# A feature-interaction tower: product arrays halved twice by accumulating DMAs, with gathers, diagonals and adds placed anew

## The chip, the cores and the metric

One core of a Trainium2 chip runs the whole program. The metric is the device time of one launch in microseconds. The kernel before takes 673.68 us, the median of three runs (673.07 to 673.69).

## What is computed

The reference looks up 39 embeddings of 16 numbers for each of 512 samples, runs three compressed-interaction layers over them, and a small network on top:

```
e  = stack(tbl_f[ids[:, f]] for f in 0..38)            # 512 x 39 x 16
X1 = einsum('hjk,bjd,bkd->bhd', W0, e, e)  + b0        # 512 x 128 x 16
X2 = einsum('hjk,bjd,bkd->bhd', W1, e, X1) + b1
X3 = einsum('hjk,bjd,bkd->bhd', W2, e, X2) + b2
z  = concat(X1.sum(2), X2.sum(2), X3.sum(2))           # 512 x 384
h  = relu(concat(z, dense_ctx) @ W_top1 + b_top1)      # 400 -> 512
h  = relu(h @ W_top2 + b_top2)                         # 512 -> 256
y  = h @ W_top3                                        # 512 x 1
```

Only the sum of X3 over d is needed, so the kernel never forms X3: it forms, for each sample, the products of x0 and X2 summed over d (called G, 39 rows and a row of plain sums), and applies W2 to those once at the end.

## The kernel before, in words

The 512 x 16 pairs of sample and d are 8192 columns. They are worked off in 16 **groups** of 512 columns (32 samples), each of four **tiles** of 128 columns (8 samples). The work of a group has two parts, and the engines run them a group apart.

**Getting embeddings and X1, one group ahead.** GpSimd adds table offsets to the ids (`index`, L317) and issues ten indirect DMAs (`gather`, L324) that fetch the rows of a group into one half of `emb`. SP (`x0_of`, L275) waits until all ten have landed, stores the rows to DRAM (L245), reads them back transposed as `rep` (L255), waits for this, and copies `rep` onto further partitions (L259). Then `factors` (L261) loads three copies as the first factor of the pair products (L268) and, one after another as VectorE uses them up, six second factors (L273), all into `shared`. SP does this in one queue in the order factors(g), x0_of(g+1), factors(g+1). While the engines work on group X, VectorE forms the seven pair products of group X+1 (`form_pairs`, L653) after the chunks in `FORM_AT` (the 7th, 11th, ... of the group's 40), TensorE multiplies them with the weights five chunks later (`pair_product`, L394), and before that, at `X0T_AT` (the ninth chunk), transposes the embeddings of group X+1 (L402). TensorE waits for `x0_loaded` of group X+1 ahead of this ninth chunk (L419). ScalarE adds the bias and splits X1 into a high and a low part; VectorE makes the low part.

**Layer two, for each tile.** W1 against X1 is 39 products of 128 columns, in ten **chunks** of up to four. Each chunk is three matmuls into one of five PSUM banks (L426 to L428). The 39 products are scaled by the embedding values: ScalarE scales six chunks (L567) and writes them into 24 arrays of `prod` (23 products and the bias row), VectorE scales four chunks (L671) and adds each into an array that ScalarE wrote. TensorE may take a bank again when the chunk in it, five chunks back, is scaled. Then 24 arrays are to be summed: when all of a tile is scaled, GpSimd issues one accumulating DMA that adds the upper twelve onto the lower twelve (`fold`, L346), and VectorE sums the twelve in four adds, 12 to 6 to 3 to 2 to 1 (`sum_over_j`, L703), at the chunks `SUM_AT`, two tiles behind (`BEHIND`). The result, X2 of the tile, is multiplied by TensorE with a block-diagonal form of the embeddings (`diag`, built by GpSimd, L334), which gives G of eight samples (`g_product`, L411), and ScalarE copies it out (L556).

GpSimd's order in a tile is: index add where there is one, wait until the previous tile is scaled, diagonal of this tile, fold of the previous tile, gathers. The ten gathers of group X+2 are spread so: nine in tiles 1 to 3 of group X-1 (`GATHERS_EARLY`, for group 2 ahead of group 0), the tenth in tile 0 of group X. The loops are unrolled by two groups, and each engine's order is written out by hand:

```
for g, half in ((odd, 1), (odd + 1, 0)):     # SP
    factors(g, half)
    x0_of(g + 1, 1 - half, at_once=False)
```

**The end.** After the last tile VectorE finishes tile 62's adds, folds tile 63 itself (`fold_last`, L685) and adds it; TensorE meanwhile runs the first top layer's products of z0 and of the dense features (L471), then those of G: W2 for j from 30 on in full precision (L491) and for the 30 others in high and low parts (L502 to L505), then the top layers (L508 to L520).

Of the kernel before, what the change touches and what calls it, by code (L numbers as in the profile page):

```python
# [53 lines left out]
LEFT = (HALF, 6, 3, 2)  # L54
BEHIND = 2
SECOND_SLOTS = 3
SLOT_USES = (BLOCKS - 1) // SECOND_SLOTS
RED = 4
# [7 lines left out]
WT1_LOADS = 3  # L66
PIECES = [(0, 3), (3, 4)]
TOP1, TOP2 = 512, 256
M1, M2 = TOP1 // P, TOP2 // P

# [4 lines left out]
GATHERS_EARLY = 9  # L75
INDEX_TILE = 1
G_AT = 2
G_COPY_AT = 5
BIAS_AT = 5
# [3 lines left out]
SUM_AT = (1, 3, 5, 7)  # L83


def tower_program(nc, ids, starts, table, dense_t, pair_a, pair_b, w1, w2, b0, b1, b2,
# [6 lines left out]
    with ctx:  # L93
# [37 lines left out]
        dense = sb("dense", [D, B])  # L131
# [62 lines left out]
        folded = [sem(f"folded{i}") for i in range(TILES_PER_GROUP)]  # L194
        last_folded = sem("last_folded")
# [28 lines left out]
        def _(sp):  # L224
# [70 lines left out]
            sp.dma_start(wt1[0:D, 3, :], top1[3 * P:, :]).then_inc(wt1_loaded, 16)  # L295
            sp.dma_start(dense[:, :], dense_t).then_inc(wt1_loaded, 16)
# [12 lines left out]
        def _(pool):  # L309
# [19 lines left out]
            def diagonal(t, slot, first):  # L329

                pool.wait_ge(x0t_ready, t + 1)
                if not first:
                    pool.wait_ge(g_mm, t - TILES_PER_GROUP + 1)
                pool.tensor_tensor(  # L334
                    diag[:, slot, :, :],
                    x0t[:, slot, :].unsqueeze(2).to_broadcast([P, J1, TB]),
                    mask[:, :].unsqueeze(1).to_broadcast([P, J1, TB]), ALU.mult).then_inc(diag_ready, 1)
# [44 lines left out]
            group(GROUPS - AHEAD - 1, 1, early=False)  # L382
            group(GROUPS - AHEAD, 0, gathers=False, early=False)
            group(GROUPS - 1, 1, gathers=False, early=False)
# [3 lines left out]
        def _(pe):  # L388
# [16 lines left out]
            def g_product(t, slot):  # L405

                pe.wait_ge(summed, (t + 1) * RED)
                pe.wait_ge(diag_ready, t + 1)
# [21 lines left out]
            def group(g, half, first=False, last=False):  # L430
                for s in range(TILES_PER_GROUP):
                    t = g * TILES_PER_GROUP + s
                    pe.wait_ge(x1_lo_ready, g * len(PIECES) + (1 if s < 3 else 2))
                    for c in range(CHUNKS):
                        p = s * CHUNKS + c
                        t_chunk(t, s, c, first and s == 0, g + 1 if p == X0T_AT and not last else None)
                        if c == G_AT and not (first and s <= BEHIND):
                            g_product(t - BEHIND - 1, (s - BEHIND - 1) % TILES_PER_GROUP)
                        if not last:
# [30 lines left out]
            def first_layer(m, rows, weights, features, start=False, stop=False):  # L470
                return pe.matmul(h1_bank[m][:, :], wt1[0:rows, weights, m * P:(m + 1) * P], features,  # L471
# [4 lines left out]
            for m in range(M1):  # L476
# [15 lines left out]
            for m in range(M1):  # L492
                first_layer(m, P, 1, G[:, F, :])
# [12 lines left out]

            pe.wait_ge(z2_ready, 1)
# [317 lines left out]
```

## Time and profile before

| | |
|---|---|
| median of three runs | 673.68 us (673.07 to 673.69) |
| the profiled execution | 672.67 us |
| its span | 670.6 us |
| TensorE matmuls busy | 641.9 us, 96% |
| VectorE busy | 521.2 us, 78% |
| ScalarE busy | 488.3 us, 73% |
| GpSimd busy | 361.1 us, 54% |
| mean granted TensorE clock | 0.995 |

The span is the profiled execution from its first to its last instruction; the time of the execution is 2.1 us longer. Matmuls are pipelined, so a matmul's row is longer than its place in the stream. In a timeline a row gives start and duration, then engine, line, operation, tile written and read, count, and in square brackets how long the engine had been idle and what released it. SPq is the DMA queue of SP; DMA_INDIRECT and DMA_DIRECT2D on POOL (GpSimd) are the times that it takes to issue them.

### The profile page before, as it was taken

How to read it: one execution, taken by the hardware profiler on the slowest of the kernel's cores; microseconds unless marked ns; L12 is line 12 of the kernel's file. 1: busy time of each engine (PE TensorE's matmuls, PEld its weight loads, DVE VectorE, ACT ScalarE, POOL GpSimd, SP SyncE). 2: the span in 40 equal slices, each digit the busy share in tenths (PEclk: the TensorE clock that was granted, in tenths of full speed). 3: DMA queues.
4: the chain of work that ended last, by engine and by line, in shares of the span. 5: the costliest groups of instructions: out<-in, count | busy, mean ns of one | idle time of the engine just before them, and what ended most of it. 6: DMA issues, size and time to landing. Idle time of an engine off the chain costs nothing.

```text
span 670.6 us, 11899 instructions
## 1 busy us (share of the span) xinstructions
PE 641.9 (96%) x2516; PEld 461.4 (69%) x2516; DVE 521.2 (78%) x1478; ACT 488.3 (73%) x1692; POOL 361.1 (54%) x308
## 2 busy tenths in 40 slices
PE   0689999999999999999999999999999999999998
PEld 0246777777777777777777777777777777785483
DVE  0346888878888888888888878888888888897590
ACT  1137877778787868787877878787868787897293
POOL 6878766575656565755666675656575221121000
PEclk9799999999999999999999999999999999999999
DMA  6457687767676777667667767676777657567100
GB/s 225 60 92 168 112 183 133 173 131 162 124 160 128 159 150 163 142 134 155 139 144 134 167 130 161 124 160 129 160 150 162 142 102 178 126 122 215 31 1 0
DMA packets 61944, 91.05 MB, mean 136 GB/s; under 512 B 34599, under 2 KB 38548, under 8 KB 61671
## 3 DMA queue, kind: packets, MB, share of 16 engines
q0 software_dynamic: 14192, 51.02, 42.0%
q1 hardware_dynamic: 47734, 39.85, 21.2%
q8 instruction: 6, 0.10, 0.1%
q14 instruction: 12, 0.09, 0.0%
HBM read 10.59 MB, written 1.28 MB: 18 GB/s over the span
## 4 chain that ended last, share of the span: by engine, by line
PE 91%; POOL 3%; DMA 3%; issue 2%; SPq 1%; ACT 0%; DVE 0%; ACTq 0%; POOLq 0%
PE t_bank L426 22%; PE t_bank L427 21%; PE t_bank L428 21%; PE x_bank L394 14%; PE small_bank L411 5%; POOL emb L324 3%; PE t_bank L491 1%; PE t_bank L471 1%; PE t_bank L502 1%; PE t_bank L503 1%; PE t_bank L514 1%; PE t_bank L505 1%; DMA emb<-in_table,idx 1%; PE x0t_bank L402 1%; DMA emb_scratch<-emb 1%
## 5 line engine op out<-in xcount | busy, mean ns | idle before, releaser
L567 ACT ACTIVATE prod<-t_bank,x0t 128x128 f32<-128x128 f32 x1472 | 417.5, 377 | 114.6 <-PE t_bank L428 109.3
L671 DVE SCALAR_TENSOR_TENSOR prod<-t_bank,x0t,prod 128x128 f32<-128x128 f32 x1024 | 287.9, 343 | 80.1 <-PE t_bank L428 75.8
L426 PE MATMUL t_bank<-w_hi,x_hi 128*128 128x512 f32 (+1 forms) x640 | 307.5, 480 | 0.6 <-DVE x_lo L660 0.3
L427 PE MATMUL t_bank<-w_lo,x_hi 128*128 128x512 f32 (+1 forms) x640 | 247.8, 387 | 0.0
L428 PE MATMUL t_bank<-w_hi,x_lo 128*128 128x512 f32 (+1 forms) x640 | 247.0, 386 | 0.0
L324 POOL DMA_INDIRECT emb<-in_table,idx x160 | 211.8, 1324 | 48.5 <-issue 46.8
L334 POOL TENSOR_TENSOR diag<-x0t,mask 128x320 f32<-128x320 f32 x64 | 87.8, 1372 | 195.4 <-DVE prod L671 97.7
L426 PEld LDWEIGHTS t_bank<-w_hi,x_hi 128*128 128x128 f32 x640 | 120.2, 188 | 54.7 <-issue 29.7
L427 PEld LDWEIGHTS t_bank<-w_lo,x_hi 128*128 128x128 f32 x640 | 120.5, 188 | 47.1 <-issue 25.3
L428 PEld LDWEIGHTS t_bank<-w_hi,x_lo 128*128 128x128 f32 x640 | 120.1, 188 | 24.2
L703 DVE TENSOR_TENSOR prod<-prod 128x768 f32<-128x768 f32 (+2 forms) x192 | 117.4, 611 | 6.0 <-DMA prod<-prod 5.7
L394 PE MATMUL x_bank<-pairs,w_pair 117*128 117x512 f32 x224 | 114.6, 594 | 2.7 <-DVE pairs L653 1.9
L653 DVE TENSOR_TENSOR pairs<-shared 117x512 f32<-117x512 f32 x96 | 65.5, 682 | 6.8 <-DMA shared<-rep 6.8
L346 POOL DMA_DIRECT2D prod<-prod x63 | 60.5, 961 | 0.0
L394 PEld LDWEIGHTS x_bank<-pairs,w_pair 117*128 117x128 f32 x224 | 41.8, 190 | 15.6 <-DVE pairs L653 6.3
L411 PE MATMUL small_bank<-diag,x 128*128 128x320 f32 x128 | 45.0, 433 | 0.0
L556 ACT ACTIVATE G<-small_bank 128x320 f32 (+1 forms) x64 | 29.1, 454 | 4.8 <-PE small_bank L411 4.8
L448 PE MATMUL t_bank<-w_pair 117*128 117x512 f32 x20 | 13.2, 816 | 16.3 <-DVE w_pair L726 16.3
L411 PEld LDWEIGHTS small_bank<-diag,x 128*128 128x128 f32 x128 | 23.9, 188 | 6.8 <-issue 0.8
L534 ACT ACTIVATE x0t<-x0t_bank 128x39 f32<-128x39 f32 x64 | 13.8, 221 | 10.7 <-PE x0t_bank L402 9.2
L542 ACT ACTIVATE x<-x_bank,bias 128x512 f32<-128x512 f32 x16 | 11.4, 715 | 13.2 <-PE x_bank L394 13.2
L625 ACT ACTIVATE w_hi<-G 128x512 fp32r<-128x512 f32 x20 | 12.6, 632 | 11.5 <-PE t_bank L505 10.5
(73 smaller groups left out, 242.8 us busy)
## 6 DMA issues: line engine op xcount, KB each, us to landing
prod<-prod POOLq DMA_DIRECT2D x63, 768.0 KB, 7.1
shared<-rep SPq DMA_DIRECT2D x96, 234.0 KB
shared<-rep SPq DMA_DIRECT2D x48, 78.0 KB
emb<-in_table,idx POOLq DMA_INDIRECT x160
G<-in_w SPq DMA_DIRECT2D x1, 2496.0 KB
rep<-rep SPq DMA_DIRECT2D x28, 78.0 KB
rep<-emb_scratch SPq DMA_DIRECT2D x20, 78.0 KB
prod<-in_w SPq DMA_DIRECT2D x1, 1536.0 KB, 7.1
```

What stands on the lines that cost most here:

```text
L324: pool.indirect_dma_start(out=emb[:, half, i * D:(i + 1) * D], out_offset=None, in_=table, in_offset=bass.IndirectOffsetOnAxis(ap=idx[:, h ...
L334: pool.tensor_tensor(diag[:, slot, :, :], x0t[:, slot, :].unsqueeze(2).to_broadcast([P, J1, TB]), mask[:, :].unsqueeze(1).to_broadcast([P, ...
L346: pool.dma_start(prod[:, slot, 0:HALF, :].rearrange("p j h -> p (j h)"), prod[:, slot, HALF:, :].rearrange("p j h -> p (j h)"), accum_op=A ...
L394: pe.matmul(x1_bank[:, :], w_pair[:, b * H:(b + 1) * H], pairs[:, b % 2, :], start=b == 0, stop=b == BLOCKS - 1).then_inc(pair_mm, 1)
L411: pe.matmul(small_bank[:, 0:TB * J1], x2[:, slot % 2, :], diag[:, slot, :, :].rearrange("p j b -> p (j b)"), start=True, stop=True).then_i ...
L426: pe.matmul(acc, hi, w1_hi[:, cols], start=True, stop=False)
L427: pe.matmul(acc, hi, w1_lo[:, cols], start=False, stop=False)
L428: pe.matmul(acc, lo, w1_hi[:, cols], start=False, stop=True).then_inc(t_mm, 1)
L567: last = act.activation(prod[:, s, SLOT[c] + u, :], t_bank[c % T_BANKS][:, u * H:(u + 1) * H], ACT.Copy, scale=x0t[:, s, j:j + 1])
L653: dve.tensor_tensor(pairs[:, b % 2, :], first, rep[0:PAIRS, half, :] if b == 0 else second[:, k, :], ALU.mult).then_inc(pair_ready, 1)
L671: last = dve.scalar_tensor_tensor(unit, t_bank[c % T_BANKS][:, u * H:(u + 1) * H], x0t[:, s, j:j + 1], unit, ALU.mult, ALU.add)
L703: dve.tensor_tensor(out, left, right, ALU.add).then_inc(summed, 1)
```

## The change

The accumulating DMA that halves 24 arrays to twelve is followed, two tiles behind, by a second one that halves twelve to six (`fold_again`); VectorE starts from six, so three adds are left, at chunks 3, 5 and 7, three tiles behind (`BEHIND` 3). The g product moves from after chunk 2 to after chunk 0. GpSimd builds each diagonal in two instructions, the second after the gathers, with a wait for the fold ahead of it. All ten gathers of group X+2 stand in group X, as 3, 3, 2, 2 in its four tiles, with the index add at the start of tile 0. In the last tile VectorE sums two tiles, and it does the last second folds itself. The dense features' product of the first top layer is put into four strips of 32 rows (row strips of the array), and one product of G is moved behind the loop over j.

```diff
-LEFT = (HALF, 6, 3, 2)
-BEHIND = 2
+QUARTER = HALF // 2
+LEFT = (QUARTER, 3, 2)
+BEHIND = 3
-RED = 4
+RED = 3
+J_SPLIT = J1 // 2
-GATHERS_EARLY = 9
-INDEX_TILE = 1
-G_AT = 2
+GATHERS_OF_TILE = [(0, 3), (3, 6), (6, 8), (8, GATHERS)]
+G_AT = 0
 G_COPY_AT = 5
+LAST_G_AT = 7
+LAST_G_COPY_AT = 9
-SUM_AT = (1, 3, 5, 7)
+SUM_AT = (3, 5, 7)
+LAST_SUM_AT = {3: ((0, 0), (0, 1)), 5: ((0, 2), (1, 0)), 7: ((1, 1), (1, 2))}
...
+            for m in range(M1):
+                strip = slice(m * STRIP, m * STRIP + D)
+                cols = slice(m * P, (m + 1) * P)
+                sp.dma_start(wt1[strip, 3, cols], top1[3 * P:, cols]).then_inc(wt1_loaded, 16)
+                sp.dma_start(dense[strip, :], dense_t).then_inc(wt1_loaded, 16)
...
-            def diagonal(t, slot, first):
-
-                pool.wait_ge(x0t_ready, t + 1)
-                if not first:
-                    pool.wait_ge(g_mm, t - TILES_PER_GROUP + 1)
+            def diagonal(t, slot, part, first):
+
+                if part == 0:
+                    pool.wait_ge(x0t_ready, t + 1)
+                    if not first:
+                        pool.wait_ge(g_mm, t - TILES_PER_GROUP + 1)
+                js = slice(0, J_SPLIT) if part == 0 else slice(J_SPLIT, J1)
...
+            def fold_again(slot):
+
+                pool.dma_start(prod[:, slot, 0:QUARTER, :].rearrange("p j h -> p (j h)"),
+                               prod[:, slot, QUARTER:HALF, :].rearrange("p j h -> p (j h)"),
+                               accum_op=ALU.add).then_inc(refolded[slot], 16)
...
-            index(AHEAD, 0)
-            for i in range(GATHERS_EARLY):
-                gather(i, 0)
-
-            def group(g, half, first=False, gathers=True, early=True):
+            def group(g, half, first=False, gathers=True, last=False):
                 for s in range(TILES_PER_GROUP):
                     t = g * TILES_PER_GROUP + s
-                    if early and s == INDEX_TILE:
-                        index(g + AHEAD + 1, 1 - half)
                     fold_before = not (first and s == 0)
+                    if gathers and s == 0:
+                        index(g + AHEAD, half)
                     if fold_before:
                         scaled(t - 1)
-                    diagonal(t, s, first)
+                    diagonal(t, s, 0, first)
                     if fold_before:
                         fold((s - 1) % TILES_PER_GROUP)
-                    if gathers and s < INDEX_TILE:
-                        for i in range(GATHERS_EARLY, GATHERS):
+                    if gathers:
+                        for i in range(*GATHERS_OF_TILE[s]):
                             gather(i, half)
-                    if early and s >= INDEX_TILE:
-                        for i in range(3 * (s - INDEX_TILE), 3 * (s - INDEX_TILE) + 3):
-                            gather(i, 1 - half)
+                    fold_twice = not (first and s < 2) and not (last and s == TILES_PER_GROUP - 1)
+                    if fold_twice:
+                        pool.wait_ge(folded[(s - 2) % TILES_PER_GROUP], (g + (1 if s >= 2 else 0)) * 16)
+                    diagonal(t, s, 1, first)
+                    if fold_twice:
+                        fold_again((s - 2) % TILES_PER_GROUP)
...
-                if m == M1 - 1:
-                    g_product(TILES - 2, 2)
-                first_layer(m, P, 0, z0[:, :], start=True)
-                first_layer(m, D, 3, dense[:, :])
-            g_product(TILES - 1, 3)
+                first_layer(m, 0, z0[:, :], start=True)
+            pe.wait_ge(diag_ready, TILES * 2)
+            g_product(TILES - 2, 3)
+            for m in range(M1):
+                strip = slice(m * STRIP, m * STRIP + D)
+                pe.matmul(h1_bank[m][:, :], wt1[strip, 3, m * P:(m + 1) * P], dense[strip, :],
+                          start=False, stop=False, tile_position=(m * STRIP, 0))
+            g_product(TILES - 1, 2)
...
-            for m in range(M1):
-                first_layer(m, P, 1, G[:, F, :])
+            for m in range(M1 - 1):
+                first_layer(m, 1, G[:, F, :])
...
+            first_layer(M1 - 1, 1, G[:, F, :])
             pe.wait_ge(z2_ready, 1)
...
+            def refold(slot):
+
+                dve.wait_ge(folded[slot], GROUPS * 16)
+                dve.tensor_tensor(prod[:, slot, 0:QUARTER, :], prod[:, slot, 0:QUARTER, :],
+                                  prod[:, slot, QUARTER:HALF, :], ALU.add).then_inc(late_refolded[slot - 1], 1)
...
-                    dve.wait_ge(folded[slot], (g + 1) * 16)
+                    dve.wait_ge(refolded[slot], (g + 1) * 16)
...
-            for i in range(RED):
-                sum_over_j(TILES - 2, GROUPS - 1, 2, i)
             fold_last(TILES - 1, 3)
             for i in range(RED):
-                sum_over_j(TILES - 1, GROUPS - 1, 3, i, by_dve=True)
+                sum_over_j(TILES - 2, GROUPS - 1, 3, i, by_dve=True)
+            refold(2)
+            for i in range(RED):
+                sum_over_j(TILES - 1, GROUPS - 1, 2, i, by_dve=True)
```

W2's loads into `prod` (L300) still wait for the sums of tiles 60 and 61, which now come at chunks 5 and 7 of the last tile; before, tile 60's came a tile earlier.

## Rows read from the trace of the kernel before

**Rows 1.** The page's part on busy time, by engine

```profile
PE 641.9 (96%) x2516; PEld 461.4 (69%) x2516; DVE 521.2 (78%) x1478; ACT 488.3 (73%) x1692; POOL 361.1 (54%) x308
```

**Rows 2.** The page's part on the chain that ended last

```profile
PE 91%; POOL 3%; DMA 3%; issue 2%; SPq 1%; ACT 0%; DVE 0%; ACTq 0%; POOLq 0%
```

**Rows 3.** Windows: stretch, busy time and instructions by engine, granted clock, DMA share, GB/s

```profile
28.00:30.00 2.00, 2.00 (x6) 1.22 (x7) 0.00 (x0) 0.49 (x4) 1.70 (x2) 0.50 0.31 45
403.30:439.30 36.00, 35.98 (x147) 26.73 (x146) 30.30 (x91) 28.47 (x105) 23.09 (x19) 1.00 0.70 147
```

**Rows 4.** Timeline of TensorE and VectorE at the start of two groups

```profile
410.31 0.32 PEld L402 LDWEIGHTS x0t_bank<-ident,rep 39*128 39x128 f32 x4 [0.35 <-issue]
...
446.30 0.32 PEld L402 LDWEIGHTS x0t_bank<-ident,rep 39*128 39x128 f32 x4 [0.35 <-issue]
...
446.64 0.68 DVE L653 TENSOR_TENSOR pairs<-shared,rep 117x512 f32<-117x512 f32 x1
...
448.69 1.02 PE L394 MATMUL x_bank<-pairs,w_pair 117*128 117x512 f32 x2
```

**Rows 5.** Timeline of GpSimd in one group

```profile
407.17 1.32 POOL L324 DMA_INDIRECT emb<-in_table,idx  x1 [0.30 <-issue]
...
431.56 1.57 POOL L334 TENSOR_TENSOR diag<-x0t,mask 128x320 f32<-128x320 f32 x1 [2.75 <-ACT prod L567]
...
433.07 0.98 POOL L346 DMA_DIRECT2D prod<-prod  x1
...
434.36 1.27 POOL L324 DMA_INDIRECT emb<-in_table,idx  x1 [0.30 <-issue]
...
435.93 1.21 POOL L324 DMA_INDIRECT emb<-in_table,idx  x1 [0.30 <-issue]
```

**Rows 6.** Timeline of SP's DMA issues in two groups

```profile
422.93 0.30 SPq L245 DMA_DIRECT2D emb_scratch<-emb  x1
...
434.93 4.24 SPq L268 DMA_DIRECT2D shared<-rep  x3
...
494.88 0.30 SPq L245 DMA_DIRECT2D emb_scratch<-emb  x1
...
508.25 2.97 SPq L268 DMA_DIRECT2D shared<-rep  x3
```

**Rows 7.** The chain in order of time, at the start

```profile
17.88 2.76 DMA emb<-in_table,idx
```

**Rows 8.** DMA queues (packets, MB, share of 16 engines) and issues

```profile
q0 software_dynamic: 14192, 51.02, 42.0%
...
prod<-prod POOLq DMA_DIRECT2D x63, 768.0 KB, 7.1
```

**Rows 9.** Timeline of the start

```profile
20.65 0.30 SPq L245 DMA_DIRECT2D emb_scratch<-emb  x1
...
27.80 2.51 SPq L268 DMA_DIRECT2D shared<-rep  x3
...
27.92 0.62 PE L402 MATMUL x0t_bank<-ident,rep 39*128 39x39 f32 x4 [5.49 <-DMA rep<-emb_scratch]
...
32.17 0.69 DVE L653 TENSOR_TENSOR pairs<-shared,rep 117x512 f32<-117x512 f32 x1 [7.23 <-DMA shared<-rep]
```

**Rows 10.** Timeline of SP and VectorE in the second group

```profile
81.06 2.37 SPq L268 DMA_DIRECT2D shared<-rep  x3
...
87.66 0.69 DVE L653 TENSOR_TENSOR pairs<-shared,rep 117x512 f32<-117x512 f32 x1 [0.58 <-DMA shared<-rep]
```

**Rows 11.** Groups of instructions by form: busy, mean ns, idle before, releaser

```profile
L703 DVE TENSOR_TENSOR prod<-prod 128x768 f32<-128x768 f32 x64 | 64.1, 1002 | 5.8 <-DMA prod<-prod 5.7
...
L334 POOL TENSOR_TENSOR diag<-x0t,mask 128x320 f32<-128x320 f32 x64 | 87.8, 1372 | 195.4 <-DVE prod L671 97.7 <-ACT prod L567 97.6
```

**Rows 12.** Timeline of the end

```profile
615.53 1.88 DVE L703 TENSOR_TENSOR prod<-prod 128x768 f32<-128x768 f32 x3 [2.41 <-DMA prod<-prod]
...
623.04 3.27 PE L491 MATMUL t_bank<-G,prod 128*128 128x512 f32 x7 [0.53 <-ACT G L556]
```

More of the change, by code:

```diff
@@ L69 @@
 M1, M2 = TOP1 // P, TOP2 // P
+STRIP = P // M1
+WT1_LOADS = 1 + 2 * M1
 FORM_AT = [6 + 4 * b for b in range(BLOCKS)]
@@ L130, in tower_program @@
         wt1 = shared
-        dense = sb("dense", [D, B])
+        dense = sb("dense", [P, B])
         w3 = sb("w3", [P, M2])
@@ L194, in tower_program @@
         folded = [sem(f"folded{i}") for i in range(TILES_PER_GROUP)]
+        refolded = [sem(f"refolded{i}") for i in range(TILES_PER_GROUP)]
+        late_refolded = [sem(f"late_refolded{i}") for i in range(2)]
         last_folded = sem("last_folded")
@@ L327, in gather @@
                 ).then_inc(gathered[half], 16)
[L329 to L333 removed]
+            def diagonal(t, slot, part, first):
[4 more added lines that the diff above has]
+                js = slice(0, J_SPLIT) if part == 0 else slice(J_SPLIT, J1)
+                n = js.stop - js.start
                 pool.tensor_tensor(
[L335 to L337 removed]
+                    diag[:, slot, js, :],
+                    x0t[:, slot, js].unsqueeze(2).to_broadcast([P, n, TB]),
+                    mask[:, :].unsqueeze(1).to_broadcast([P, n, TB]), ALU.mult).then_inc(diag_ready, 1)
             def scaled(t):
@@ L381, in _ @@
                     group(g, half)
-            group(GROUPS - AHEAD - 1, 1, early=False)
-            group(GROUPS - AHEAD, 0, gathers=False, early=False)
-            group(GROUPS - 1, 1, gathers=False, early=False)
+            group(GROUPS - AHEAD - 1, 1)
+            group(GROUPS - AHEAD, 0, gathers=False)
+            group(GROUPS - 1, 1, gathers=False, last=True)
         @block.tensor
@@ L407, in g_product @@
                 pe.wait_ge(summed, (t + 1) * RED)
[L408 removed]
+                pe.wait_ge(diag_ready, (t + 1) * 2)
                 if not (isinstance(t, int) and t == 0):
@@ L438, in group @@
                             g_product(t - BEHIND - 1, (s - BEHIND - 1) % TILES_PER_GROUP)
+                        if last and s == TILES_PER_GROUP - 1 and c == LAST_G_AT:
+                            g_product(t - BEHIND, 0)
                         if not last:
@@ L466, in _, with first_layer @@
             g_product(TILES - 3, 1)
-            def first_layer(m, rows, weights, features, start=False, stop=False):
-                return pe.matmul(h1_bank[m][:, :], wt1[0:rows, weights, m * P:(m + 1) * P], features,
+            def first_layer(m, weights, features, start=False, stop=False):
+                return pe.matmul(h1_bank[m][:, :], wt1[:, weights, m * P:(m + 1) * P], features,
                                  start=start, stop=stop)
@@ L584, in group @@
                             copy_g(t - BEHIND - 1, g if s > BEHIND else g - 1, (s - BEHIND - 1) % TILES_PER_GROUP)
+                        if last and s == TILES_PER_GROUP - 1 and c == LAST_G_COPY_AT:
+                            copy_g(t - BEHIND, g, 0)
                         if not last:
@@ L684, in fold_last @@
                 dve.wait_ge(dve_scaled, (t + 1) * ND)
-                dve.tensor_tensor(prod[:, slot, 0:HALF, :], prod[:, slot, 0:HALF, :], prod[:, slot, HALF:, :],
-                                  ALU.add).then_inc(last_folded, 1)
+                for i, n in enumerate((HALF, QUARTER)):
+                    if i > 0:
+                        dve.wait_ge(last_folded, i)
+                    dve.tensor_tensor(prod[:, slot, 0:n, :], prod[:, slot, 0:n, :], prod[:, slot, n:2 * n, :],
+                                      ALU.add).then_inc(last_folded, 1)
             def sum_over_j(t, g, slot, i, by_dve=False):
@@ L721, in group @@
                         if c in SUM_AT and not (first and s < BEHIND):
-                            sum_over_j(t - BEHIND, g if s >= BEHIND else g - 1, (s - BEHIND) % TILES_PER_GROUP,
-                                       SUM_AT.index(c))
+                            if last and s == TILES_PER_GROUP - 1:
+                                for slot, i in LAST_SUM_AT[c]:
+                                    if (slot, i) == (1, 0):
+                                        refold(slot)
+                                    sum_over_j(t - BEHIND + slot, g, slot, i, by_dve=slot == 1)
+                            else:
+                                sum_over_j(t - BEHIND, g if s >= BEHIND else g - 1, (s - BEHIND) % TILES_PER_GROUP,
+                                           SUM_AT.index(c))
             dve.wait_ge(w_loaded, 16 * 3)
```

17 lines of the change are left out of this document (8 added, 9 removed).

## The prediction, made before the changed kernel had run

> **What bounds the kernel now.** I read the busy shares first, then the chain of waits. TensorE is busy for 96% of the span and carries 91% of the chain [rows 1, 2]. The clock, busy times and DMA share of one group of four tiles (403.3 to 439.3 us) come next: TensorE 35.98 of 36 us at full clock, VectorE 30.30, GpSimd 23.09, the DMA engines 0.70 [rows 3]. The transposes of two successive groups start at 410.31 and 446.30, so a group lasts 35.99 us, and that is TensorE's own work [rows 4]. The first thing to carry along: taking work off VectorE can't shorten such a group. The second: everything that must be ready at a fixed place in TensorE's order has a margin, and a change that eats the margin makes TensorE wait. So I looked for the margins.
>
> **The margin of the next group's embeddings.** While group X runs, the gathers for X+2 finish, SP stores the rows to DRAM, reads them back transposed, copies them within SBUF, and loads three copies as first factors. Their users stand in group X+1: TensorE's transposes after its ninth chunk (446.30), VectorE's first pair product (446.64), TensorE's first matmul on it (448.69) [rows 4]. Before the change, the last gather for X+2 is issued early in group X, at 407.17 [rows 5]; SP's store goes out at 422.93 (it waits for SP's turn, not for the gather), the first-factor loads at 434.93 [rows 6]. That is nearly 12 us ahead of 446.64.
>
> **Part by part.**
>
> *Gathers.* The diff takes away the nine gathers issued ahead of group 0 and the index add in tile 1, and issues the ten gathers of X+2 as 3, 3, 2, 2 in the four tiles of group X. The last is no longer in tile 0 but in tile 3, and the store of SP needs all ten. Where does it land? GpSimd enters tile 3 at 431.56, released by the tile before; nothing of that moves. Then half the diagonal, 0.75 (half of 431.56 to 433.07), the fold's issue with the gap behind it 1.29 (433.07 to 434.36), the first gather 1.57 (434.36 to 435.93) [rows 5], and from the start of the last gather to its landing 2.76 [rows 7]: 431.56 + 6.37 = 437.9. Those gathers stand behind a fold on the same software queue, whose landing is 7.1 us from issue [rows 8], that is 432.3 + 7.1 = 439.4. No row shows whether a gather waits for the fold ahead of it: bounds 0 and 1.8 us; I take 1.0, so 438.9.
>
> The Trainium skill, page "DMA: Bandwidth & Descriptors", section on the anatomy of one DMA, gives a software-queue DMA a fixed 2.0 us plus its bytes over 436 GB/s. By that a 768 KB fold lands in an estimated 3.8 us, the gather would not be held, and the sum would be 14 us lower. The 7.1 us of the row disagree, and the row decides.
>
> *From store to first-factor loads.* 12.0 us (422.93 to 434.93) in one group, 13.4 (494.88 to 508.25) in another [rows 6]. I take 13.4, because a second fold now falls in the same stretch: loads go out at 452.3.
>
> *From there to the first pair product.* 4.4 us with quiet queues (27.80 to 32.17) [rows 9], 6.6 between folds (81.06 to 87.66) [rows 10]; middle, 5.5: 457.8. The product takes 0.7: TensorE can run its matmul at 458.5 where it ran it at 448.69. **9.8 us late.**
>
> *Does it all reach TensorE?* Yes: its queue is in order. It stops before its ninth chunk for the embeddings (some 6 us), runs three chunks, and stops again at the pair matmul. VectorE stands at the pair product with the scaling of chunk 8 behind it, ScalarE has the transposed embeddings to copy; nothing can overtake. During such a stop the clock falls: after 5.49 us of idleness ahead of 27.92 TensorE had a granted clock of 0.50, that is 1.2 GHz [rows 3, 9]. The three chunks then take some 2 us more, mostly inside the second wait; I add 0.2, between 0 and 1. Per group 10.0, between 6.3 (437.9 + 12.0 + 4.4 + 0.7) and 12.7 (439.7 + 13.4 + 6.6 + 0.7, plus 1).
>
> *How often?* The next tile 3 is released by TensorE's later work, so the loss is paid anew in every group that prepares a successor gathered in the loop: groups 1 to 14, 14 times. 14 x 10.0 = 140 us, between 88 and 178.
>
> *Second fold.* 61 more DMA issues on GpSimd, 0.98 us each by the fold's row [rows 5]; GpSimd goes from 23.09 to about 27.0 us a group, under 36 [rows 3]: hidden. Where a tile has three gathers it is issued 7.6 us after GpSimd enters the tile (0.75 + 1.29 + 3 x 1.57 + a second half 0.8), and asked for at VectorE's fourth chunk of the next, about 12.6 after (tiles of 9.0 us, chunks of 0.9). Half the bytes, so its landing takes between 2.2 (the share of the rings alone, below) and 7.1 us, middle 4.6: 12.2. VectorE waits between 0 and 2.1 us. TensorE runs up to four chunks, 3.6 us, ahead of it in its five banks, which covers that: 0. If that cover is gone: rival 2. Ring time: the software queue's 42% of 670.6 us is at most 4.5 us for each of 63 folds [rows 8], so half-size ones add at most 2.2 a tile, 9 a group: 25.2 + 9 = 34 of 36 us. This is why I take the upper value above.
>
> *VectorE adds.* The 768-wide add goes, 1.00 us, 61 times [rows 11]. Worth nothing, since VectorE was hidden. The g product after chunk 0 comes three chunks after the last add; TensorE does the same work: 0.
>
> *Diagonal in two.* 1.37 us on GpSimd becomes twice about 0.8 [rows 11]: hidden, 0. The x0t copies of ScalarE wait for the second half, done 7.6 us after GpSimd's entry, and want it early in the next tile, 9.0 after: 0.
>
> *Head.* Nine gathers fewer beside the second group's loads: 0, between -1 and 0.
>
> *Tail.* VectorE waited 2.41 us for the last DMA fold before its adds at 615.53, and the z2 matmuls began at 623.04 [rows 12]. New: tiles 60 and 61 are added inside the last tile, tile 63 before tile 62, dense products in strips, one first-layer product moved under a wait. Against it, W2's first load starts one tile later and meets the second. I take -1.5, between -4 (most of those waits gone) and +2.
>
> **Sum.** 672.7 (the profiled execution, span 670.6 and 2.1 around it) + 140 - 1.5 = 811.2; the median of the runs is 1.0 above the profiled one: **812 us**.
>
> **Rivals.**
> 1. *The chain runs as on quiet queues.* While TensorE stands still, fewer loads compete. 11.5 us from store to pair product (20.65 to 32.17) [rows 9]: 437.9 + 11.5 + 0.7 = 450.1, 1.4 late, 14 times 20 us: 692; mixtures reach 755. For it: the pause empties the rings. Against: the software queue alone takes 42% of the engines' time [rows 8], and the folds of tiles 2 and 3 are in it during the pause. 10%.
> 2. *The folds fill the rings.* On top of the forecast, pair loads and second folds come late in tiles 1 to 3, another 3 us a group: 42 more, 854, up to 900 at 6. For it: 34 of 36 us. Against: the longer group gives the rings 46. 4%.
> 3. *The embeddings are in time after all, and the change is faster.* It decides at 446.6: the whole path from landed gather to pair product must fit in 8.7 us, where the shortest seen is 11.5. Price: the tail's -4 to -1.5: 669 to 672. 4%.
> 4. *In time, and the tail gives nothing:* 673 to 675. 2%.
>
> **How the numbers follow.** The forecast has 80%, with 758 (88 and -3) to 853 (178 and +2). The range 755 to 855 leaves out 20% at most. A measurement of this kernel can tell about 0.2%, 1.3 us: faster 0.04, same 0.02, slower 0.94.
>
> **What would show it.** In the changed profile: group period near 46 us where it was 35.99; SP's store just behind the last gather of tile 3, released by the gather's DMA; TensorE idle before the transposes, released by the copies of rep, and before the first pair matmul; VectorE idle before the first pair product, released by the first-factor loads; 14 of each; a granted clock near 0.5 behind each pause. TensorE's busy share falls to some 80%. It is wrong if the transposes keep a period of 36 us; a step is wrong if the store comes after 440 (relative to a tile 3 entered at 431.56), or the waits are found at the folds.

## The result, and the profile after

The changed kernel takes 835.39 us (median of 4, 832.03 to 836.37) beside 673.68 us (median of 4, 673.07 to 677.39) for the kernel before: ratio 1.238, 95% interval 1.234 to 1.243. The forecast was 812, so the direction held, the main mechanism too, and 23 us were missing. A run more than 1.5% above the fastest of its kernel counts as slow and stays out of the ratios; below, these are one of e1 (729.86 us) and one of e5 (734.30 us). The profiled execution took 835.56 us with a span of 833.7, which is 162.9 us above the 672.7 of before.

The page of the changed kernel: busy shares, the chain by engine, the software queue (packets, MB, share), and the two halving DMAs (KB each, median us from issue to landing).

```profile
PE 692.8 (83%) x2516; PEld 488.1 (59%) x2516; DVE 463.4 (56%) x1417; ACT 491.4 (59%) x1692; POOL 395.9 (47%) x433
...
PE 48%; DMA 33%; SPq 6%; issue 5%; POOL 5%; DVE 2%; ACT 0%; DVEq 0%; POOLq 0%
...
q0 software_dynamic: 22976, 75.01, 49.9%
...
prod<-prod POOLq DMA_DIRECT2D x63, 768.0 KB, 6.4
prod<-prod POOLq DMA_DIRECT2D x61, 384.0 KB, 4.4
```

TensorE falls from 96% of the span to 83%, and DMAs and SP's issues take 39% of the chain where they had 4% [rows 1, 2]. VectorE has indeed lost its work (56% busy), and nobody profits.

Its waits (us in total, times, longest us):

```profile
PE t_bank L444 <- DMA rep<-rep: 105.9, 14, 8.5
...
DVE pairs L679 <- DMA shared<-rep: 156.8, 22, 11.1
...
PE small_bank L429 <- DVE x L740: 5.7, 15, 1.0
```

Fourteen times TensorE stops for the embeddings ahead of its transposes, 7.6 us each. The third row is a wait that the forecast didn't have, short but with something behind it.

One group, followed from GpSimd's entry into tile 3, E = 406.07. GpSimd first (start, us):

```profile
406.07 0.45 POOL L347 TENSOR_TENSOR diag<-x0t,mask 128x160 f32<-128x160 f32 x1 [2.82 <-PE small_bank L429]
406.52 0.92 POOL L359 DMA_DIRECT2D prod<-prod  x1
...
409.33 1.26 POOL L334 DMA_INDIRECT emb<-in_table,idx  x1 [0.30 <-issue]
```

The chain in order of time from there, and SP's issues in this group and the next:

```profile
409.33 3.79 DMA emb<-in_table,idx
413.34 3.10 DMA emb_scratch<-emb
416.61 6.77 DMA rep<-emb_scratch
...
425.06 2.21 DMA rep<-rep
```

```profile
413.34 0.30 SPq L252 DMA_DIRECT2D emb_scratch<-emb  x1
...
427.28 2.38 SPq L275 DMA_DIRECT2D shared<-rep  x3
...
475.05 2.38 SPq L275 DMA_DIRECT2D shared<-rep  x3
```

SP stores right behind the last gather, at E + 7.27, and loads the first factors 13.94 us later. The same loads of the next group come 47.8 us on; before, a group lasted 35.99 [rows 4]. Then TensorE and VectorE (in brackets the idle time before and what ended it):

```profile
427.49 0.79 PE L444 MATMUL t_bank<-w_hi,x_hi 128*128 128x512 f32 x1 [7.52 <-DMA rep<-rep]
...
431.39 0.69 DVE L679 TENSOR_TENSOR pairs<-shared,rep 117x512 f32<-117x512 f32 x1 [10.04 <-DMA shared<-rep]
...
432.00 0.28 DVE L740 TENSOR_TENSOR x<-prod 128x128 f32<-128x128 f32 x1
...
432.53 1.41 PE L429 MATMUL small_bank<-diag,x 128*128 128x320 f32 x2 [0.29 <-DVE x L740]
...
435.02 1.40 PE L412 MATMUL x_bank<-pairs,w_pair 117*128 117x512 f32 x2
```

and windows of the group (columns as in [rows 3]):

```profile
403.30:451.10 47.80, 39.97 (x148) 28.82 (x147) 26.66 (x87) 28.59 (x104) 24.82 (x27) 0.86 0.71 143
...
427.40:429.50 2.10, 2.02 (x7) 1.28 (x7) 0.00 (x0) 0.00 (x0) 0.00 (x0) 0.50 0.14 38
433.50:435.50 2.00, 2.00 (x5) 1.37 (x5) 0.42 (x1) 0.42 (x3) 1.31 (x2) 0.50 0.31 103
```

The pair product starts at E + 25.3, and its matmul at E + 28.95, where before it stood at 448.69 - 431.56 = E + 17.13 [rows 4, 5]: 11.8 us late. Between pair product and matmul lie not 0.7 but 3.63 us: VectorE's last add (432.00), the g product that waits for it (432.53) and a whole chunk, both of these at a granted clock of 0.50. Before the change the g product stood two chunks later, behind the pair matmul. 14 x 11.8 = 165 us against 162.9 in all; the rest lies in the tail, which is 1.3 us shorter (below), and in the head and the uneven first groups, which were not separated.

### The profile page after: what moved, and what is told of

Read it like the earlier page. It is cut to its first block, busy times and chain, and to the rows that moved or that the text cites. A ratio compares the mean times of both kernels' runs of the same rounds, so it can differ in the third digit from the quotient of the medians.

```text
span 833.7 us, 11983 instructions
## 1 busy us (share of the span) xinstructions
PE 692.8 (83%) x2516; PEld 488.1 (59%) x2516; DVE 463.4 (56%) x1417; ACT 491.4 (59%) x1692; POOL 395.9 (47%) x433
## 4 chain that ended last, share of the span: by engine, by line
PE 48%; DMA 33%; SPq 6%; issue 5%; POOL 5%; DVE 2%; ACT 0%; DVEq 0%; POOLq 0%
DMA rep<-emb_scratch 12%; PE t_bank L444 10%; PE t_bank L445 10%; PE t_bank L446 10%; PE x_bank L412 9%; DMA emb<-in_table,idx 7%; DMA emb_scratch<-emb 5%; DMA shared<-rep 5%; PE small_bank L429 4%; DMA rep<-rep 4%; SPq L275 3%; SPq L266 3%; POOL emb L334 2%; POOL prod L359 2%; PE t_bank L514 1%
## 5 line engine op out<-in xcount | busy, mean ns | idle before, releaser
L444 PE MATMUL t_bank<-w_hi,x_hi 128*128 128x512 f32 (+1 forms) x640 | 326.1, 510 | 106.5 <-DMA rep<-rep 105.9
L445 PE MATMUL t_bank<-w_lo,x_hi 128*128 128x512 f32 (+1 forms) x640 | 259.5, 405 | 0.0
L446 PE MATMUL t_bank<-w_hi,x_lo 128*128 128x512 f32 (+1 forms) x640 | 258.2, 403 | 0.0
L347 POOL TENSOR_TENSOR diag<-x0t,mask 128x160 f32<-128x160 f32 x128 | 68.8, 537 | 324.9 <-PE small_bank L429 278.6
L445 PEld LDWEIGHTS t_bank<-w_lo,x_hi 128*128 128x128 f32 x640 | 128.6, 201 | 48.1 <-issue 28.0
L446 PEld LDWEIGHTS t_bank<-w_hi,x_lo 128*128 128x128 f32 x640 | 127.9, 200 | 26.2
L679 DVE TENSOR_TENSOR pairs<-shared,rep 117x512 f32<-117x512 f32 x16 | 11.1, 695 | 152.6 <-DMA shared<-rep 152.6
L365 POOL DMA_DIRECT2D prod<-prod x61 | 62.8, 1030 | 0.0
L429 PE MATMUL small_bank<-diag,x 128*128 128x320 f32 x128 | 53.8, 505 | 7.6 <-DVE x L740 5.7
L359 POOL DMA_DIRECT2D prod<-prod x63 | 57.0, 905 | 0.2 <-issue 0.2
L740 DVE TENSOR_TENSOR prod<-prod 128x384 f32<-128x384 f32 (+1 forms) x128 | 54.8, 428 | 0.2
L558 ACT ACTIVATE x0t<-x0t_bank 128x39 f32<-128x39 f32 x64 | 13.7, 219 | 11.8 <-PE x0t_bank L420 11.5
```

The costliest lines, as they stand in the source:

```text
L347: pool.tensor_tensor(diag[:, slot, js, :], x0t[:, slot, js].unsqueeze(2).to_broadcast([P, n, TB]), mask[:, :].unsqueeze(1).to_broadcast([P ...
L359: pool.dma_start(prod[:, slot, 0:HALF, :].rearrange("p j h -> p (j h)"), prod[:, slot, HALF:, :].rearrange("p j h -> p (j h)"), accum_op=A ...
L365: pool.dma_start(prod[:, slot, 0:QUARTER, :].rearrange("p j h -> p (j h)"), prod[:, slot, QUARTER:HALF, :].rearrange("p j h -> p (j h)"), ...
L429: pe.matmul(small_bank[:, 0:TB * J1], x2[:, slot % 2, :], diag[:, slot, :, :].rearrange("p j b -> p (j b)"), start=True, stop=True).then_i ...
L444: pe.matmul(acc, hi, w1_hi[:, cols], start=True, stop=False)
L445: pe.matmul(acc, hi, w1_lo[:, cols], start=False, stop=False)
```

## The experiments

All ratios are against the kernel before, run on the same chip beside the others of its set. Two theories stood at first: the late gathers carry nearly everything (the forecast's), or folds and the placement of g product and adds carry a part of their own.

**e1: the changed kernel with the gathers placed as before**

```diff
-GATHERS_OF_TILE = [(0, 3), (3, 6), (6, 8), (8, GATHERS)]
+GATHERS_EARLY = 9
+INDEX_TILE = 1
...
+            index(AHEAD, 0)
+            for i in range(GATHERS_EARLY):
+                gather(i, 0)
...
+                    if gathers and s < INDEX_TILE:
+                        for i in range(GATHERS_EARLY, GATHERS):
                             gather(i, half)
+                    if early and s >= INDEX_TILE:
+                        for i in range(3 * (s - INDEX_TILE), 3 * (s - INDEX_TILE) + 3):
+                            gather(i, 1 - half)
```

> The changed kernel with the gathers placed as before (nine of ten a group earlier, the tenth in tile 0), all else of the change kept. Theory A (the late gathers make the whole loss): no wait for the copies of rep before the ninth chunk, group period back to 36.0 us, time between 668 and 673 us. Rival B (the second fold and its load on the DMA rings carry part of the loss): the period stays at 37 us or more and the time is above 685 us; the folds' landing times then grow over the 6.4 and 4.4 us of the changed kernel.

Measured: 706.7 us (6 runs; 706.63 over the five in the ratio), ratio 1.047, 1.043 to 1.052. So 129 of 162 us go with the gathers, and 33 stay. TensorE's waits, and SP's timeline, of e1:

```profile
PE small_bank L437 <- DVE x L748: 23.9, 12, 5.1
```

```profile
405.19 1.14 SPq L253 DMA_DIRECT2D emb_scratch<-emb  x1
...
422.64 2.38 SPq L276 DMA_DIRECT2D shared<-rep  x3
```

No wait for the embeddings is left. The one that remains is at the g product, and SP's chain takes 17.45 us where it took 12.0 and 13.4 [rows 6]. The second fold is not the only possible cause of that: see e6 and e12.

**e2: the kernel before with the gathers placed as in the change, and nothing else**

```diff
-GATHERS_EARLY = 9
-INDEX_TILE = 1
+GATHERS_OF_TILE = [(0, 3), (3, 6), (6, 8), (8, GATHERS)]
...
+                    if gathers and s == 0:
+                        index(g + AHEAD, half)
...
+                    if gathers:
+                        for i in range(*GATHERS_OF_TILE[s]):
                             gather(i, half)
```

> The kernel before with only the ten gathers placed as in the change (3, 3, 2, 2 in the four tiles, one fold, whole diagonal, g product after chunk 2). Theory A: nearly the whole loss; last gather issued 4.4 us after GpSimd's entry into tile 3, landed at 8.2, loads of the first factors 13 us later, pair product 4.8 after that, 26.0 in place of 17.1: 8.9 us a group and some 0.3 for the clock, 14 times 9.2, about 802 us (790 to 815). Rival B (the second fold matters): under 760 us. The difference to the changed kernel, some 33 us, is then the g product ahead of the pair product and the second fold.

Measured: 804.33 us (2 runs), ratio 1.193, 1.188 to 1.198. The edit alone costs 130 us, as expected. TensorE's wait, and SP's timeline, of e2:

```profile
PE t_bank L418 <- DMA rep<-rep: 94.4, 14, 8.1
```

```profile
443.41 0.30 SPq L244 DMA_DIRECT2D emb_scratch<-emb  x1
...
455.98 2.38 SPq L267 DMA_DIRECT2D shared<-rep  x3
```

Store to loads takes 12.6 us here, without a second fold.

**e3: the changed kernel with the ten gathers in tiles 0 to 2**

```diff
-GATHERS_OF_TILE = [(0, 3), (3, 6), (6, 8), (8, GATHERS)]
+GATHERS_OF_TILE = [(0, 4), (4, 7), (7, GATHERS), (GATHERS, GATHERS)]
```

> The changed kernel with the ten gathers in tiles 0 to 2 as 4, 3, 3. Theory A: the last gather is issued 7.7 us earlier relative to TensorE's stream, so of the 10.2 us by which the first pair product is late 2.5 are left, the wait before the ninth chunk is gone, and the clock stays up: 14 times 2.5 to 3, about 708 us (700 to 716). If the loss did not hang on the place of the last gather, it stays above 800 us.

Measured: 815.07 us (2 runs), ratio 1.209, 1.203 to 1.216: a plain miss. SP's timeline of e3, where GpSimd enters tile 3 at 446.59:

```profile
445.55 0.30 SPq L252 DMA_DIRECT2D emb_scratch<-emb  x1
...
464.18 2.94 SPq L275 DMA_DIRECT2D shared<-rep  x3
```

The store does come 8.3 us earlier, at E - 1.04. But store to loads takes 18.6 us (18.3 to 20.1 in all 14 groups) instead of 13.9, so that the loads come only 3.6 us earlier, at E + 17.6. The likely reason, not tested by itself, is that most of the chain now runs while TensorE works and folds are issued, and not in TensorE's pause. 3.6 x 14 would be 50 us and the time fell by 20; where the other 30 go was not followed up, except that TensorE's wait at the g product has grown to 19.3 us in all (5.7 in the changed kernel). The chain's length isn't a constant that can be carried from place to place; that is the first hint at the folds.

**e4: the changed kernel with 32 matmuls that nobody reads, ahead of the wait for the embeddings**

```diff
+WARM = 32
...
-                    pe.wait_ge(x0_loaded, (then_x0t + 1) * (16 * X0_LOADS))
                     pe.wait_ge(x0t_ready, then_x0t * TILES_PER_GROUP)
+                    for _ in range(WARM):
+                        pe.matmul(x0t_bank[:, :], x1_hi[:, s * P:(s + 1) * P], w1_hi[:, 0:COLS], start=True, stop=True)
+                    pe.wait_ge(x0_loaded, (then_x0t + 1) * (16 * X0_LOADS))
```

> The changed kernel with 32 dummy matmuls of 512 columns (7.4 us) in the transposes' bank just ahead of the wait for the embeddings, so that TensorE is busy while it would wait. Theory A (the second wait is mostly VectorE's pair product and the add behind it, the low clock costs about 1.3 us a group): granted clock 1.0 throughout, 14 times 1.3 less, about 817 us. If the clock carries the whole 2.9 us between the expected and the measured distance from pair product to its matmul: 795 us. If it carries nothing: 835 us.

Measured: 842.81 us (2 runs), ratio 1.250, 1.245 to 1.256. TensorE's timeline of e4:

```profile
427.91 7.42 PE L440 MATMUL x0t_bank<-w_hi,x_hi 128*128 128x512 f32 x32
435.48 0.49 PE L447 MATMUL t_bank<-w_hi,x_hi 128*128 128x512 f32 x1
...
440.62 1.41 PE L430 MATMUL small_bank<-diag,x 128*128 128x320 f32 x2 [2.39 <-DVE x L743]
```

The dummies fill the pause and the chunks behind it run at full speed, but then TensorE waits 2.39 us for VectorE's add. The period is 47.8 us as without them, and the difference of 7.4 us fits the 7.42 us of dummies once more, in the first group, which had no pause to fill. So the slow clock behind the first pause costs nothing. The second stretch of low clock is not tested: behind the wait of 2.39 us the g product again takes 1.41 us, at a granted clock of 0.50.

**e5: e1 with the g product after chunk 2**

```diff
-G_AT = 0
+G_AT = 2
```

> The changed kernel with early gathers and the g product after chunk 2, as before the change, the second fold kept. Theory C: the first factors stay late, but TensorE reaches the first pair matmul, which needs only the pair product, ahead of the g product, which needs the add behind it; about 2 us less in each of the ten groups that waited, 680 to 695 us. Rival D: the g product's place is all of it, 669 to 675 us. If its place costs nothing: 703 to 710 us.

Measured: 722.61 and 734.30 us; with one run left no ratio is given. The first lies above the five runs in e1's ratio (702.95 to 710.44), though, so moving the g product back is no remedy here with the second fold in place, as far as one run shows. The only profile is of the run of 734.30 us. In it the wait at the g product is nearly gone (1.0 us in all), but TensorE waits 26.2 us before pair matmuls and VectorE 67.4 us for folds. A possible reason is that GpSimd's diagonal waits for the g product, so that a later g product makes the second fold later; this and its size are left open.

**e6: e1 with the second halving done by VectorE**

```diff
-                    if fold_twice:
-                        pool.wait_ge(folded[(s - 2) % TILES_PER_GROUP], (g + (1 if s >= 2 else 0)) * 16)
                     diagonal(t, s, 1, first)
-                    if fold_twice:
-                        fold_again((s - 2) % TILES_PER_GROUP)
...
-                    dve.wait_ge(refolded[slot], (g + 1) * 16)
+                    dve.wait_ge(folded[slot], (g + 1) * 16)
+                    dve.tensor_tensor(prod[:, slot, 0:QUARTER, :], prod[:, slot, 0:QUARTER, :],
+                                      prod[:, slot, QUARTER:HALF, :], ALU.add).then_inc(dve_refolded, 1)
```

> The changed kernel with the gathers early (as in the first experiment, 706.7 us) and, besides, the second halving done by VectorE (a 768-wide add ahead of the three others, still three tiles behind) in place of the 61 accumulating DMAs. Theory C (the 33 us that are left with early gathers come from the second fold's load on the DMA rings, which stretches SP's chain for the embeddings and makes the first factors late): the DMA share falls from 0.9 to 0.7, the period is 36.0 us in every group, no first pair product waits, 669 to 673 us. Rival D (they come from the new order: g product after chunk 0, three tiles behind, half diagonals): still above 695 us.

Measured: 700.5 us (6 runs), ratio 1.036, 1.031 to 1.041. Taking the second fold away gives only 6 of the 33 us (7 or 8 by the ratios), so most of e1's loss is elsewhere. The timeline of e6 at the start of a group:

```profile
470.81 0.69 DVE L684 TENSOR_TENSOR pairs<-shared,rep 117x512 f32<-117x512 f32 x1
471.42 0.28 DVE L748 TENSOR_TENSOR x<-prod 128x128 f32<-128x128 f32 x1
...
471.74 1.14 ACT L596 ACTIVATE prod<-t_bank,x0t 128x128 f32<-128x128 f32 x4 [0.92 <-DVE x L748]
...
471.95 0.78 PE L434 MATMUL small_bank<-diag,x 128*128 128x320 f32 x2 [1.35 <-DVE x L748]
```

Here is the rest. With adds at chunks 3, 5 and 7, the last add of tile t-4 stands behind the pair product at the end of tile t-1. The g product of that tile follows one chunk later on TensorE, and ScalarE's first scaling of tile t, which takes the same one of four `prod` slots, waits for the same add.

**e7: the changed kernel (late gathers) with the second halving done by VectorE.** The edit is that of e6, on the changed kernel.

> The changed kernel, gathers late as changed, with the second halving done by VectorE. If the second fold slows the chain from the last gather to the pair product also here: some 1 us less a group, 815 to 825 us. If the wait of TensorE empties the rings anyway: 830 to 836 us, as the changed kernel.

Measured: 785.04 us (2 runs), ratio 1.162, 1.153 to 1.171, lower than expected. SP's timeline of e7:

```profile
433.24 0.30 SPq L253 DMA_DIRECT2D emb_scratch<-emb  x1
...
443.95 2.38 SPq L276 DMA_DIRECT2D shared<-rep  x3
```

GpSimd enters this tile 3 at 425.75, so the store is at E + 7.49, near the 7.27 of the changed kernel, and the loads follow after 10.7 us (10.4 to 10.9 in most groups) instead of 13.9. 3.2 us x 14 = 45 of the 50 us by which the second fold lengthens the changed kernel.

**e8: the changed kernel with the g product after chunk 2.** The edit is that of e5, on the changed kernel.

> The changed kernel, gathers late and second fold kept, with the g product after chunk 2. The pair matmul no longer stands behind the g product and one more chunk at the low clock, 2.2 us less in 14 groups; against it GpSimd's diagonal waits for this g product, so it enters each tile some 1 us later and the last gather with it. About 824 us (815 to 830). If the place of the g product costs nothing here: 835 us or more.

Measured: 837.45 us (2 runs), ratio 1.239, 1.230 to 1.248: no gain. TensorE's wait for the embeddings in e8:

```profile
PE t_bank L444 <- DMA rep<-rep: 124.9, 14, 9.9
```

The wait for VectorE's add before the g product is gone from the list, and this one has grown by 19 us. GpSimd's diagonal in tile 3 waits for the g product, and the gathers stand behind it. So what the pair matmul gains, the chain gives back: first-factor loads still come every 47.8 us.

**e9: e6 with the g product after chunk 2**, the edit of e5 again.

> Early gathers, second halving on VectorE, g product after chunk 2, adds after chunks 3, 5, 7. Theory E: TensorE's own wait vanishes, ScalarE's for the prod slot stays, about 0.9 us at each start of tile 1, which the five banks should cover: 669 to 678 us. If ScalarE's wait is the one that counts: 690 us or more.

Measured: 672.93 us (10 runs), ratio 0.999, 0.996 to 1.001.

**e11: e6 with the adds at chunks 1, 3 and 5**

```diff
-SUM_AT = (3, 5, 7)
-LAST_SUM_AT = {3: ((0, 0), (0, 1)), 5: ((0, 2), (1, 0)), 7: ((1, 1), (1, 2))}
+SUM_AT = (1, 3, 5)
+LAST_SUM_AT = {1: ((0, 0), (0, 1)), 3: ((0, 2), (1, 0)), 5: ((1, 1), (1, 2))}
```

> Early gathers, second halving on VectorE (as the run of 700.5 us), and VectorE's adds after chunks 1, 3, 5 in place of 3, 5, 7, all else as changed. Theory E (the 26 us of that run come from the last add of a tile: TensorE's g product and ScalarE's first chunk, which takes the tile's prod slot over, stand right behind it): both waits vanish, period 36.0 us, 669 to 673 us. Rival F (half diagonals, the g product's place or the diagonal's wait for it): still above 690 us.

Measured: 672.38 us (12 runs) beside 673.58, ratio 0.997, 0.995 to 0.999, the fastest version here, at the edge of what a measurement tells. TensorE's wait at the g product in e11:

```profile
PE small_bank L434 <- DVE x L748: 0.2, 1, 0.2
```

20.6 us in 17 waits (e6) became 0.2 in one. Either edit (the add two chunks earlier, the g product two chunks later) takes back the whole loss of e6: 28 us between the medians, 25 to 26 by the ratios. In e9 only the g product has moved and the add stands where it stood in e6, yet ScalarE's idle time for it falls from 13.1 us to 1.1. So it was TensorE's wait at the g product that counted, and ScalarE's followed from it.

**e10: the kernel before with the tail's edits alone**

```diff
+STRIP = P // M1
...
-                if m == M1 - 1:
-                    g_product(TILES - 2, 2)
                 first_layer(m, P, 0, z0[:, :], start=True)
-                first_layer(m, D, 3, dense[:, :])
+            g_product(TILES - 2, 2)
+            for m in range(M1):
+                strip = slice(m * STRIP, m * STRIP + D)
+                pe.matmul(h1_bank[m][:, :], wt1[strip, 3, m * P:(m + 1) * P], dense[strip, :],
+                          start=False, stop=False, tile_position=(m * STRIP, 0))
```

> The kernel before with two pieces of the change's end alone: the dense products in four row strips and one of the first layer's G products behind the loop over j. The moved product fills TensorE's wait for z2 (0.9 us); the strips free 3 us of TensorE ahead of the last two g products, of which VectorE's adds leave 0 to 1: 0.9 to 1.9 us faster than before, 672 to 673 us, within the measurement's noise or just outside. If neither counts: no difference.

Measured: 674.56 us (12 runs), ratio 1.000, 0.998 to 1.002. TensorE's timeline of e10 at the end:

```profile
617.85 0.81 PE L415 MATMUL small_bank<-diag,x 128*128 128x320 f32 x2 [1.20 <-DVE x L710]
618.59 0.69 PE L488 MATMUL x_bank<-dense,shared 16*128 16x512 f32 x1
618.60 0.69 PE L488 MATMUL x0t_bank<-dense,shared 16*128 16x512 f32 x1
618.60 0.70 PE L488 MATMUL t_bank<-dense,shared 16*128 16x512 f32 x2
...
621.76 1.15 PE L415 MATMUL small_bank<-diag,x 128*128 128x320 f32 x2 [2.03 <-DVE x L710]
623.43 10.70 PE L497 MATMUL t_bank<-G,prod 128*128 128x512 f32 x18 [0.53 <-ACT G L563]
```

and, for comparison, the last of these rows in the kernel before:

```profile
623.04 7.99 PE L491 MATMUL t_bank<-G,prod 128*128 128x512 f32 x18 [0.53 <-ACT G L556]
```

The strips work: four products run at once. But the time goes into waits of 1.20 and 2.03 us for VectorE's last adds, which the dense products had covered, and behind the second wait the granted clock is 0.50 (from 624 to 628 us). The 18 products of G that follow take 10.70 us where they took 7.99. These 2.7 us are more than the 0.9 that the moved product saves. In the changed kernel, where VectorE's adds are placed differently, the last wait is 0.22 us and the 18 products take 7.99.

**e12: e11 with one accumulating DMA of 296 KB a tile that nobody reads**

```diff
+LOAD_COLS = 592
...
+                    if loads:
+                        pool.dma_start(load[:, :], w1_lo[:, 0:LOAD_COLS].bitcast(f32), accum_op=ALU.add).then_inc(load_done, 16)
```

> The 672.4 us version (early gathers, halving on VectorE, adds after chunks 1, 3, 5) with one accumulating DMA more per tile at the place of the second fold, 296 KB (three quarters of it) onto a scratch array that nobody reads: the second fold's load on the DMA rings by itself, with no one waiting for it. Theory C, corrected (the load alone stretches SP's chain for the embeddings, and makes the first factors late): DMA share 0.85, store to first-factor loads 15 to 17 us in place of 12 to 13, VectorE waits for the first factors and TensorE 1 to 1.5 us at the first pair matmul in most groups, 680 to 692 us. If the load alone is hidden: 671 to 675 us.

Measured: 690.74 us (4 runs), ratio 1.024, 1.020 to 1.028. The waits of e12 on TensorE and VectorE:

```profile
PE x_bank L431 <- DVE pairs L698: 14.6, 15, 3.6
```

```profile
DVE pairs L698 <- DMA shared<-rep: 53.8, 20, 8.5
```

Nobody waits for the load itself. But from 380 to 640 us the DMA engines are busy 85% of the time (64% in e11), SP's store to loads takes 17.3 to 17.8 us in nearly every group (in e11 11.7 to 15.5 from the fifth group on, and 16.7 to 17.5 in the first four), and the pair product is late: 18 us for three quarters of the second fold's bytes. VectorE waits 2.1 to 3.2 us for the first factors in 13 of 14 groups and 5.5 us in the last; in e11 it waits so in three. So the added DMA has a price of its own, through SP's queue and not through whoever waits for the fold. That it is the transfers and not the 61 further issues on GpSimd is likely but not separated. And the DMA share alone doesn't set the chain's length: in e6, at 0.64 and without any second fold, store to loads also takes 16.0 to 17.0 us in 13 of 14 groups, but nearly every pair product there finds its loads landed.

## Why the prediction was right, and where it was short

- *Last gather and store.* Forecast E + 7.34, measured E + 7.27. The last gather is issued at E + 3.26 and not 3.61, lands 3.79 us later where 2.76 + 1.0 were taken, and SP's store follows 0.2 us behind, which hadn't been counted. The stated bound of 1.8 us for the wait behind the fold is a slip: 439.4 - 437.9 is 1.5.
- *Store to loads.* 13.4 against 13.94, with 13.5 to 14.4 in all groups. The choice of the upper row for the second fold's sake went the right way; e7 shows 10.7 without that fold. That it came within 0.5 us has luck in it: with the second fold the same stretch took 18.6 in e3, without it 12.6 in e2, and nothing in the forecast tells these apart.
- *Loads to pair product.* 5.5 against 4.11, near the 4.4 of the quiet start [rows 9].
- *Reaches TensorE, paid anew in 14 groups.* Shown: e2 has the 14 waits and 130 us with this edit alone, and e1 loses the waits with its undoing. The prediction was right for this reason.
- *Pair product to its matmul: the mis-sized term.* "The product takes 0.7", and "the g product after chunk 0 comes three chunks after the last add: 0". The three chunks hold for all tiles but the one that counts: there TensorE's queue has stopped and VectorE's last add stands behind the late pair product. The forecast also lets three chunks pass and puts the pair matmul next; behind the third comes the g product, and then a fourth chunk. Measured 3.63 us instead of 0.9 with the clock's 0.2: 2.7 x 14 = 38 us too few, of which the smaller loads-to-product term gives back 19; the longer store to loads adds 8. Together that is the step from 10.0 to 11.8 us a group. With early gathers the same placement costs 25 to 28 us (e6 against e9 and e11). That it can't be bought back in the changed kernel by moving the g product alone (e8) wasn't foreseen either: the diagonal and the gathers stand behind it.
- *Second fold: "0", wrong in kind.* VectorE's waits for it were looked at, the ring time was worked out (34 of 36 us) and then used only to choose a row. By e12 the load of one more DMA a tile costs 18 us, by e1 against e6 the second fold 6, by the changed kernel against e7 it costs 50. The costs don't add up: what is already late hides what gets late beside it.
- *Clock.* 0.2 us were taken for the chunks in the second wait. By e4 the low clock behind the first pause costs nothing. It does cost something inside the 3.63 us, at a g product and a chunk; this is read from the rows and not tested by a run: 432.53 to 435.02 takes 2.49 us, where the same pieces at full clock, 0.55 and 0.70 in this kernel's chain, make some 1.25.
- *Signs named ahead.* Period near 46: 47.8. TensorE's share near 80%: 83%. SP's store before E + 8.4, released by the gather: seen. A long TensorE wait before the first pair matmul: not seen; the slow chunks fill it, and a wait of 0.29 us stands at the g product instead.
- *Tail, -1.5.* From the start of the last tile's first chunk to the end of the span it is 65.4 us before (605.21 to 670.6) and 64.1 after (769.61 to 833.7): -1.3 in the profiled executions, close to the forecast. e10 holds only two of the tail's pieces and says nothing measurable: between -1.3 and +1.5 us. There the strips' gain turned into waits for VectorE and slow products behind them.
- *Rivals.* The quiet chain (692 to 755) is refuted: loads to pair product did run as on quiet queues, store to loads did not. Of the second rival (folds fill the rings, 854 and up), the waits that it names didn't come: the 96 later pair products waited 4.2 us for their loads in all. A price of DMA load exists (e12), and in the changed kernel it is contained in the 13.9. The two rivals that have the embeddings in time fall with the 14 waits.

What stays open: why early gathers with second fold and a late g product (e5) come out above e1, since only one of its runs counts and the profile is of the other; and how much of e1's 33 us belongs to each of the two causes, since each hides part of the other (33 together, 25 to 28 for the placement alone in e6, 18 for three quarters of the second fold's load alone in e12). Open too is what sets the length of SP's chain, which ran from 10.0 to 20.1 us in these kernels.

## What to carry to other kernels

For every wait at a fixed place in an in-order engine, write down the margin, and recompute it for the worst tile of the period, not the usual one: here the "three chunks" of slack were real in three tiles of four and absent in the fourth. A DMA that nobody waits for still has a price where the DMA engines are two thirds busy, namely in the length of other queues' dependent chains; look at those before calling it hidden. And when a part of the change helps an engine that isn't the bound, as the second fold helps VectorE, its side effects are all that is left of it.

## What the runs showed of the hardware

An accumulating DMA within SBUF of 384 KB landed in 4.4 us, the one of 768 KB in 6.4, in the changed kernel; with the DMA engines 87% busy (e1, from 380 to 640 us) they took 7.8 and 7.2. The share doesn't decide this alone: in e5, at 85%, they took 5.4 and 7.1. The Trainium skill, page "DMA: Bandwidth & Descriptors", section on the anatomy of one DMA, would put them at an estimated 2.9 and 3.8 us (2.0 fixed plus bytes over 436 GB/s); no run's median is below 4.4 and 6.2 (e2). No run here has such a DMA on quiet queues, so for accumulating DMAs between other traffic the estimate is at best a floor.

A gather issued behind a fold on the software queue landed in 3.79 us, against 2.76 at the quiet start [rows 7]. It landed at 413.12, and the fold, issued at 406.52, by its median of 6.4 us at some 412.9: whether the gather is held until the fold has landed, or only shares the engines with it, these rows don't tell.

Four matmuls of 16 rows in four strips of the array start within 0.01 us (618.59 to 618.60) and, in two passes, take 1.1 us together in e10, where the four products took about 1.06 us each one after the other before.
